# Two gated layers in one matmul stream: the second layer's tiles taken in turns with the first layer's later products

## The chip, the cores and the metric

The kernel runs on one NeuronCore of a Trainium2 chip. The metric is device time in microseconds (us) of one execution; lower is better. Engines are called as in the profile: PE (TensorE, the matrix engine), PEld (its weight loads), DVE (VectorE), ACT (ScalarE), POOL (GpSimd), SP (SyncE, which issues the DMAs here).

## The reference

Eight batches of 512 tokens with 512 features pass a gated feed-forward net twice: with weights of an expert that the batch's label picks, and with shared weights. The two results are mixed with two weights per batch and added to the input.

```python
def ffn(x, wi0, wi1, wo):                     # 512 -> 2048 -> 512
    return gelu(x @ wi0) * (x @ wi1) @ wo
share_out  = ffn(x, sWi0, sWi1, sWo)
expert_out = ffn(x, Wi0[label], Wi1[label], Wo[label])     # per batch
gate_in = concatenate([expert_out[:, 0], share_out[:, 0]])
w = softmax(relu(gate_in @ g0) @ g1)
return x + expert_out * w[:, 0] + share_out * w[:, 1]
```

All of it is float32.

## The kernel before

**Split operands.** A float32 operand is kept as a high part (a rounding to fp32r, made by ACT) and a low part (the rest, made by DVE as a difference). A product takes three passes: low by high, high by low, high by high (PASSES).

**Seven products.** The first layer (x by wi0, called GATE, and x by wi1, called LIN) is computed as a two-by-two block product with seven block products instead of eight (P1 to P7, in the order P5, P1, P6, P2, P7, P3, P4 of their storage). The sums of weight blocks that it needs are made by DVE (weight_sums, L948 to L956). The results are put together in PSUM and on DVE: c11 is P1 + P2; c22 and c12 are ps_v and ps_p5 with a saved P5 added (L1044, L1048); c21 is P4 on top of a copy of ps_v (copy_u, L821).

**Steps and passes.** The hidden width of 2048 is walked in 8 steps of 256. Batches go in pairs, and a pair is 24 steps: 8 expert steps of the first batch, 8 shared steps for both batches at once, 8 expert steps of the second batch. There are 4 pairs. An expert step is one turn, with matmuls 256 columns wide. A shared step has two turns, a GATE turn and then a LIN turn, with matmuls 512 columns wide (wide_product, L427): 6 of them in each product.

**Second layer.** What a step produced, the hidden block, is multiplied by wo one step later. Its four row tiles (down, L436) are 6 matmuls of 512 columns each, into the four banks of ps_outs. In the shared steps the GATE turn takes the tiles of one batch and the LIN turn those of the other (shared_tile); DVE adds each tile to s_out (add_tile, L1063). The first shared step of a pass still owes the last expert step's tiles; they go in its LIN turn (expert_tile), and ACT copies them out (L738).

**Before the hidden block can be used** in step n it must be split: DVE multiplies the last quarter that needs P4 of the LIN turn (c21_product, L1020), ACT makes the high part (hid_hi, L703), DVE the low part (hid_lo, L931, hidl), and that raises hid_ready. PE waits for hid_ready(n) in front of the first tile of the step.

**Order.** Each engine runs its own list, written out by hand, in order, with semaphores between the lists. For a LIN turn DVE's list is (shared_lin): c11 product, c22, c12, the product of act and lin (L1218), the low part of the next step's weights, group 0 (a_lo(n+1, 0), 128x2048), four adds, the low part of group 1 (a_lo(n+1, 1), 128x1024). For a GATE turn (shared_gate): c21_product of the turn before, weight_sums 0 and 1, hid_lo, weight_sums 2, a_lo of group 2, c22, c12, four adds, the low part of wo. P1 of a step waits for a_ready of group 0 of its weights. P7 waits for v_copied, a copy that ACT makes after P6, and P4 for u_copied, one that ACT makes after P7.

**On SP** the loads of weights (next_a, next_wo) wait for a_ready and wo_ready of the step, and load for the step two or one later.

Of the kernel before, what the change touches and what calls it, by code (L numbers as in the profile page):

```python
# [19 lines left out]
GATE, LIN = 0, 1  # L20
# [29 lines left out]
def first_turn(n):  # L50
    pair, q = divmod(n, PAIR_STEPS)
    return pair * PAIR_TURNS + (q if q < STEPS else 2 * q - STEPS if q < 2 * STEPS else q + STEPS)
# [25 lines left out]
def downs(t):  # L78


    return 4 * t - (4 if WIDE0 <= t % PAIR_TURNS < EXPERT1 else 0)
# [16 lines left out]
def a_splits(m, g):  # L98


    return 5 if m == 0 else m * 3 + (g + (5 if m == 1 else 6))
# [7 lines left out]
def x_splits(b, g):  # L109

    return 8 if b == 0 else b * 3 + (g + 6)


def build(nc, x_cols, x_rows, labels, experts, shared, g0_rows, g1_rows, out):
# [3 lines left out]
    MC = TOK // P  # L118
# [9 lines left out]
    with ExitStack() as ctx:  # L128
# [3 lines left out]
        def sem(name):  # L132
            return ctx.enter_context(nc.semaphore(name))
# [58 lines left out]
        def halves(ps):  # L192
            return ps.rearrange("p (a t) -> p a t", a=2)
# [23 lines left out]
        wo_ready = sem("wo_ready")  # L217
# [15 lines left out]
        hid_ready = sem("hid_ready")  # L233
# [177 lines left out]
        def _(pe):  # L411
# [11 lines left out]
            def wide_product(i, a, ps, start):  # L423

                for k in range(2):
                    for q, (ap, xp) in enumerate(PASSES):
                        mm = nc.tensor.matmul(ps, a_op[ap][:, i, a, k, :],  # L427
                                              x_op[xp][:, i, k, :, :].rearrange("p h t -> p (h t)"),
                                              start=(start and k == 0 and q == 0), stop=(k == 1 and q == 2),
                                              skip_group_check=True)  # L430
                return mm

            def down(m, s, start, stop, hidden):
                for f in range(2):
                    for q, (hp, wp) in enumerate(PASSES):
                        mm = nc.tensor.matmul(ps_out[m], hidden[hp][:, f, m * P:(m + 1) * P], wo[s][wp][:, f, :],  # L436
                                              start=(start and f == 0 and q == 0), stop=(stop and f == 1 and q == 2),
                                              skip_group_check=True)
                return mm
# [40 lines left out]
            def c11_taken(t):  # L480
                if is_gate(t):
                    pe.wait_ge(gelu_done, gelus(t) + 1)
                else:
                    pe.wait_ge(product_done, products(t) + 1)

            def expert_tile(m, b, n):

                c = n % STEPS
                start = c == 0
                if c == 0 and b == BATCH - 1:  # L490

                    pe.wait_ge(negative_copied, m + 1)
                    start = False
                elif c == 0 and b % 2 == 1:

                    pe.wait_ge(added, (b // 2 + 1) * PAIR_ADDS - MC + (m + 1))
                elif c == 0 and b > 0:

                    pe.wait_ge(out_copied, (b - 1) * MC + (m + 1))
                down(m, n % 2, start, c == STEPS - 1, hidden_of[0]).then_inc(down_done, 1)  # L500

            def shared_tile(m, h, b, n):

                row = n % STEPS * 2 + h
                if row == 0:

                    pe.wait_ge(out_copied, b * MC + (m + 1))
                else:

                    pe.wait_ge(added, b // 2 * PAIR_ADDS + row * MC - MC + (m + 1))  # L510
                down(m, n % 2, True, True, hidden_of[h]).then_inc(down_done, 1)
# [54 lines left out]
            def shared_turn(n, c, b, a):  # L566

                t = first_turn(n) + a
                if a == GATE:
                    pe.wait_ge(a_ready, a_splits(n, 0))  # L570
                    if c == 0:
                        pe.wait_ge(x_ready, x_splits(b + 1, 2))
                c11_taken(t - 1)
                wide_product(P1, a, ps_c11[:, :], True).then_inc(p_done[P1], 1)
                pe.wait_ge(c12_done, t - 1)
                wide_product(P5, a, ps_p5, True).then_inc(p_done[P5], 1)
                pe.wait_ge(p1_copied, t)
                wide_product(P6, a, ps_v, False).then_inc(p_done[P6], 1)
                wide_product(P2, a, ps_c11[:, :], False).then_inc(p_done[P2], 1)
                if a == GATE:  # L580
                    pe.wait_ge(a_ready, a_splits(n, 1))
                pe.wait_ge(v_copied, t)
                wide_product(P7, a, ps_v, False).then_inc(p_done[P7], 1)
                wide_product(P3, a, ps_p5, False).then_inc(p_done[P3], 1)

                if a == (GATE if c > 0 else LIN):
                    pe.wait_ge(hid_ready, n)
                    pe.wait_ge(wo_ready, n)
                for m in range(MC):
                    if c > 0:  # L590
                        shared_tile(m, a, b, n - 1)
                    elif a == LIN:
                        expert_tile(m, b, n - 1)
                if a == GATE:
                    pe.wait_ge(a_ready, a_splits(n, 2))
                pe.wait_ge(u_copied, t)
                wide_product(P4, a, ps_c21[:, :], False).then_inc(p_done[P4], 1)
# [19 lines left out]
            n, t, b = N_STEPS - 1, N_TURNS - 1, BATCH - 1  # L617
# [311 lines left out]
        def _(dve):  # L929
# [60 lines left out]
            def hid_lo(n):  # L990
                dve.wait_ge(hid_hi_done, n + 1)
                if is_wide(n):
                    lo(hs[LO][:, :, :, :], act[:, :, :, :], hs[HI][:, :, :, :], hid_ready)
                else:
                    lo(hs[LO][:, 0, :, :], act[:, LIN, :, :], hs[HI][:, 0, :, :], hid_ready)
# [17 lines left out]
            def c21_product(t):  # L1013

                if is_gate(t):
                    return
                if is_lin(t):
                    dve.wait_ge(gelu_done, gelus(t))
                    dve.wait_ge(p_done[P4], t)
                    nc.vector.tensor_tensor(act[:, :, 1, 0:HALF], act[:, :, 1, 0:HALF], halves(ps_c21[:, :]), ALU.mult  # L1020
                                            ).then_inc(product_done, 1)
                else:
                    dve.wait_ge(gelu_done, gelus(t) + 3)
                    nc.vector.tensor_tensor(act[:, LIN, 1, 0:HALF], act[:, GATE, 1, 0:HALF], ps_c21[:, HALF:2 * HALF],
                                            ALU.mult).then_inc(product_done, 1)
# [15 lines left out]
            def c22(t, to):  # L1041
                dve.wait_ge(u_copied, t)
                dve.wait_ge(p5_saved, t)
                nc.vector.tensor_tensor(to, halves(ps_v), p5[:, :, :], ALU.add).then_inc(c22_done, 1)  # L1044

            def c12(t, to):
                dve.wait_ge(p_done[P3], t)
                nc.vector.tensor_tensor(to, halves(ps_p5), p5[:, :, :], ALU.add).then_inc(c12_done, 1)  # L1048

            def add_tile(m, h, b, n, t, skip):  # L1050


                dve.wait_ge(down_done, downs(t) - skip - MC + (m + 1))
                to = s_out[:, h, m, :]
                if n % STEPS == 0:
                    if b > 0:

                        dve.wait_ge(out_stored, (b - 2 + h) * 16 + 16)
                    nc.vector.tensor_copy(to, ps_out[m]).then_inc(added, 1)
                else:  # L1060

                    dve.wait_ge(added, b // 2 * PAIR_ADDS + (n % STEPS * 2 + h - 2) * MC + (m + 1))
                    nc.vector.tensor_tensor(to, to, ps_out[m], ALU.add).then_inc(added, 1)  # L1063
# [128 lines left out]
            def shared_gate(n, c, b):  # L1192
                t = first_turn(n)
                c21_product(t - 1)
                weight_sums(n + 1, 0)
                weight_sums(n + 1, 1)
                hid_lo(n - 1)
                weight_sums(n + 1, 2)
                a_lo(n, 2)
                dve.wait_ge(hid_ready, n)  # L1200
                c22(t, act[:, :, 1, HALF:TOK])
                c12(t, act[:, :, 0, HALF:TOK])
                if c > 0:
                    for m in range(MC):
                        add_tile(m, 0, b, n - 1, t, 0)
                wo_lo(n)

# [188 lines left out]
```

## Time and profile before

| | |
|---|---|
| median of 3 runs | 1965.66 us (1965.66 to 1966.04) |
| span of the profiled execution, first to last instruction | 1964.4 us |
| PE busy | 1959.5 us, 11159 matmuls |
| DVE busy | 1525.0 us |
| ACT busy | 1038.3 us |
| POOL busy | 81.8 us |
| DMA, mean | 99 GB/s |

The profiled execution is known by its span; the 1.26 us between it and the median of the runs lie around the first and last instruction. Times in the trace are counted from the span's start. A matmul's duration in the trace has its pipeline's tail in it, so neighbours overlap: what a matmul costs is the distance from its start to the next one's. The same holds for other engines' instructions, which start up to 0.1 us before the one ahead ends.

### The profile page before, as it was taken

What the parts mean: (1) busy time and instruction counts of PE and PEld (TensorE: products, weight loads), DVE (VectorE), ACT (ScalarE), POOL (GpSimd) and SP (SyncE); (2) the same over time, 40 slices, a digit from 0 to 9 for tenths busy, and PEclk for the clock granted to TensorE, in tenths of its full rate; (3) what the DMA queues carried; (4) which work ended last, traced back from release to release, by engine and by line L of the source; (5) the groups of instructions that cost most, each with busy time, mean ns of one, the idle gap of its engine ahead of it and who ended that gap; (6) DMA issues with size and microseconds to landing.
All of it is one profiled execution on the core that took longest, in us unless ns stands there. A gap on an engine that the chain in (4) does not pass through costs nothing.

```text
span 1964.4 us, 29030 instructions
## 1 busy us (share of the span) xinstructions
PE 1959.5 (100%) x11159; PEld 1728.9 (88%) x11159; DVE 1525.0 (78%) x1814; ACT 1038.3 (53%) x1379; POOL 81.8 (4%) x56
## 2 busy tenths in 40 slices
PE   9999999999999999999999999999999999999999
PEld 8988888899998888889999888889999988888998
DVE  8776667789887676778988767668898876766888
ACT  6564444466666444446666644344666664434564
POOL 0000000001010000000201000000010100000000
PEclk9999999999999999999999999999999999999999
DMA  5431111244452111124445311112444421111243
GB/s 161 144 103 54 59 49 54 68 158 140 144 181 84 61 52 49 55 86 140 155 146 167 97 49 54 47 62 76 155 152 145 162 92 49 54 54 54 79 163 113
DMA packets 152428, 194.83 MB, mean 99 GB/s; under 512 B 10466, under 2 KB 116962, under 8 KB 150498
## 3 DMA queue, kind: packets, MB, share of 16 engines
q1 hardware_dynamic: 151746, 192.46, 30.2%
q8 instruction: 88, 1.44, 0.3%
q10 hardware_dynamic: 544, 0.52, 0.1%
q14 instruction: 50, 0.41, 0.1%
HBM read 184.55 MB, written 8.39 MB: 98 GB/s over the span
## 4 chain that ended last, share of the span: by engine, by line
PE 99%; DVE 1%; issue 0%; ACT 0%; DVEq 0%; ACTq 0%
PE ps_outs L436 35%; PE ps_pv L417 18%; PE ps_pv L427 18%; PE ps_c L417 13%; PE ps_c L427 13%; PE ps_c L458 0%; PE ps_pv L611 0%; DVE al L931 0%; PE ps_outs L417 0%; PE ps_outs L458 0%; PE ps_outs L445 0%; DVE a_src L952 0%; DVE xl L931 0%; DVE hidl L931 0%; DVE a_src L948 0%
## 5 line engine op out<-in xcount | busy, mean ns | idle before, releaser
L931 DVE TENSOR_TENSOR al<-a_src,ah 128x1024 fp32r<-128x1024 f32 (+3 forms) x293 | 402.0, 1374 | 34.3 <-ACT ah L659 33.7
L659 ACT CAST ah<-a_src 128x1024 fp32r<-128x1024 f32 (+2 forms) x285 | 334.9, 1187 | 0.5 <-DVE a_src L952 0.5
L417 PE MATMUL ps_pv<-xh,al 128*128 128x256 f32 x1008 | 285.4, 283 | 0.2 <-ACT ps_pv L815 0.2
L417 PE MATMUL ps_pv<-xl,ah 128*128 128x256 f32 x1008 | 285.3, 283 | 0.0
L417 PE MATMUL ps_pv<-xh,ah 128*128 128x256 f32 x1008 | 285.3, 283 | 0.0
L716 ACT ACTIVATE act<-ps_c 128x256 f32<-128x256 f32 (+1 forms) x191 | 87.1, 456 | 308.3 <-PE ps_c L417 170.6
L806 ACT COPY ps_pv<-ps_c 128x512 f32<-128x512 f32 x127 | 72.5, 571 | 268.0 <-PE ps_c L427 182.1
L417 PE MATMUL ps_c<-xh,ah 128*128 128x256 f32 x756 | 213.9, 283 | 0.0
L417 PE MATMUL ps_c<-xl,ah 128*128 128x256 f32 x756 | 213.9, 283 | 0.0
L417 PE MATMUL ps_c<-xh,al 128*128 128x256 f32 x756 | 213.6, 283 | 0.0
L436 PE MATMUL ps_outs<-wo0h,hidl 128*128 128x512 f32 x512 | 199.6, 390 | 0.0
L436 PE MATMUL ps_outs<-wo0l,hidh 128*128 128x512 f32 x512 | 199.6, 390 | 0.0
L427 PE MATMUL ps_pv<-xh,al 128*128 128x512 f32 x512 | 199.4, 389 | 0.0
L427 PE MATMUL ps_pv<-xl,ah 128*128 128x512 f32 x512 | 199.2, 389 | 0.0
L427 PE MATMUL ps_pv<-xh,ah 128*128 128x512 f32 x512 | 199.2, 389 | 0.0
L436 PE MATMUL ps_outs<-wo0h,hidh 128*128 128x512 f32 x512 | 199.2, 389 | 0.0
L1063 DVE TENSOR_TENSOR s_out<-s_out,ps_outs 128x512 f32<-128x512 f32 x224 | 146.1, 683 | 67.6 <-PE ps_outs L436 67.3
L436 PE MATMUL ps_outs<-wo1h,hidl 128*128 128x512 f32 x504 | 196.5, 390 | 0.0
L436 PE MATMUL ps_outs<-wo1l,hidh 128*128 128x512 f32 x504 | 196.4, 390 | 0.0
L436 PE MATMUL ps_outs<-wo1h,hidh 128*128 128x512 f32 x504 | 196.1, 389 | 0.0
L417 PEld LDWEIGHTS ps_pv<-xh,al 128*128 128x128 f32 x1008 | 193.5, 192 | 0.6 <-issue 0.5
L417 PEld LDWEIGHTS ps_pv<-xl,ah 128*128 128x128 f32 x1008 | 193.5, 192 | 0.1
(131 smaller groups left out, 3943.2 us busy)
## 6 DMA issues: line engine op xcount, KB each, us to landing
a_src<-experts SPq DMA_DIRECT2D x255, 256.0 KB, 3.7
raw_wo<-experts SPq DMA_DIRECT2D x128, 256.0 KB, 2.8
a_src<-shared SPq DMA_DIRECT2D x128, 256.0 KB, 3.0
g_sb<-g_rows SPq DMA_DIRECT2D x16, 1024.0 KB, 5.4
raw_wo<-shared SPq DMA_DIRECT2D x64, 256.0 KB, 2.8
x_src<-x_cols SPq DMA_DIRECT2D x30, 256.0 KB, 3.9
g_sb<-x_rows SPq DMA_DIRECT2D x7, 1024.0 KB, 4.8
out<-s_out SPq DMA_DIRECT2D x7, 1024.0 KB, 7.2
```

Of the source, the lines that this page charges most:

```text
L417: mm = nc.tensor.matmul(ps[:, a * HALF:(a + 1) * HALF], a_op[ap][:, i, a, k, :], x_op[xp][:, j, k, h, :], start=(start and a == 0 and k == ...
L427: mm = nc.tensor.matmul(ps, a_op[ap][:, i, a, k, :], x_op[xp][:, i, k, :, :].rearrange("p h t -> p (h t)"), start=(start and k == 0 and q ...
L436: mm = nc.tensor.matmul(ps_out[m], hidden[hp][:, f, m * P:(m + 1) * P], wo[s][wp][:, f, :], start=(start and f == 0 and q == 0), stop=(sto ...
L659: nc.scalar.copy(a_op[HI][:, i:j, :, :, :], a_src[m % 2][:, i:j, :, :, :]).then_inc(a_hi_done, 1)
L716: nc.scalar.activation(to, of, ACT.Gelu_apprx_tanh).then_inc(gelu_done, 1)
L806: nc.scalar.copy(ps_v, ps_c11[:, :]).then_inc(p1_copied, 1)
L931: nc.vector.tensor_tensor(to, of, hi.bitcast(F32), ALU.subtract).then_inc(done, 1)
L1063: nc.vector.tensor_tensor(to, to, ps_out[m], ALU.add).then_inc(added, 1)
```

## The change

In shared steps PE's order changes from P1 P5 P6 P2 P7 P3 T0 T1 T2 T3 P4 to P1 P5 P6 P2 **T0** P7 **T1** P3 **T2 T3** P4 (T0 to T3 are the tiles of the second layer; in the GATE turn of the first shared step of a pass there are none). The waits for hid_ready and wo_ready move with T0. DVE's list of a GATE turn takes the add of tile 0 between c22 and c12; its list of a LIN turn stays as it is.

```diff
+                def tile(m):
+
+                    if a == (GATE if c > 0 else LIN) and m == 0:
+                        pe.wait_ge(hid_ready, n)
+                        pe.wait_ge(wo_ready, n)
+                    if c > 0:
+                        shared_tile(m, a, b, n - 1)
+                    elif a == LIN:
+                        expert_tile(m, b, n - 1)
+
                 wide_product(P2, a, ps_c11[:, :], False).then_inc(p_done[P2], 1)
+                tile(0)
                 if a == GATE:
                     pe.wait_ge(a_ready, a_splits(n, 1))
                 pe.wait_ge(v_copied, t)
                 wide_product(P7, a, ps_v, False).then_inc(p_done[P7], 1)
+                tile(1)
                 wide_product(P3, a, ps_p5, False).then_inc(p_done[P3], 1)
-
-                if a == (GATE if c > 0 else LIN):
-                    pe.wait_ge(hid_ready, n)
-                    pe.wait_ge(wo_ready, n)
-                for m in range(MC):
-                    if c > 0:
-                        shared_tile(m, a, b, n - 1)
-                    elif a == LIN:
-                        expert_tile(m, b, n - 1)
+                tile(2)
+                tile(3)
                 if a == GATE:
                     pe.wait_ge(a_ready, a_splits(n, 2))
                 pe.wait_ge(u_copied, t)
@@ shared_gate, on DVE
                 c22(t, act[:, :, 1, HALF:TOK])
+                if c > 0:
+                    add_tile(0, 0, b, n - 1, t, 0)
                 c12(t, act[:, :, 0, HALF:TOK])
                 if c > 0:
-                    for m in range(MC):
+                    for m in range(1, MC):
                         add_tile(m, 0, b, n - 1, t, 0)
                 wo_lo(n)
```

## Rows read from the trace of the kernel before

**Rows 1.** The page: PE's busy time, and its granted clock in 40 slices.

```profile
PE 1959.5 (100%) x11159; PEld 1728.9 (88%) x11159; DVE 1525.0 (78%) x1814; ACT 1038.3 (53%) x1379; POOL 81.8 (4%) x56
...
PEclk9999999999999999999999999999999999999999
```

**Rows 2.** Waits of PE: waiting line, releaser, us in total, times, longest.

```profile
PE ps_pv L611 <- DVE idle L1280: 1.2, 1, 1.2
PE ps_pv L417 <- ACT ps_pv L815: 0.2, 1, 0.2
```

**Rows 3.** Timeline of PE, a LIN turn and the next GATE turn: start, duration.

```profile
226.00 0.39 PE L427 MATMUL ps_c<-xh,al 128*128 128x512 f32 x1
...
233.94 0.39 PE L427 MATMUL ps_pv<-xh,ah 128*128 128x512 f32 x1
234.16 0.39 PE L436 MATMUL ps_outs<-wo0h,hidl 128*128 128x512 f32 x1
...
240.96 0.39 PE L427 MATMUL ps_c<-xh,al 128*128 128x512 f32 x1
...
246.40 0.39 PE L427 MATMUL ps_pv<-xh,al 128*128 128x512 f32 x1
...
249.12 0.39 PE L436 MATMUL ps_outs<-wo1h,hidl 128*128 128x512 f32 x1
```

**Rows 4.** Timeline of DVE in the same stretch.

```profile
234.36 0.69 DVE L1048 TENSOR_TENSOR lin<-ps_pv,p 128x512 f32<-128x512 f32 x1
235.14 1.23 DVE L1218 TENSOR_TENSOR act<-act,lin 128x1024 f32<-128x1024 f32 x1
236.29 2.28 DVE L931 TENSOR_TENSOR al<-a_src,ah 128x2048 fp32r<-128x2048 f32 x1
238.49 2.47 DVE L1063 TENSOR_TENSOR s_out<-s_out,ps_outs 128x512 f32<-128x512 f32 x4
240.88 1.22 DVE L931 TENSOR_TENSOR al<-a_src,ah 128x1024 fp32r<-128x1024 f32 x1
242.01 0.68 DVE L1020 TENSOR_TENSOR act<-act,ps_c 128x512 f32<-128x512 f32 x1
...
243.33 1.22 DVE L952 TENSOR_TENSOR a_src<-a_src 128x1024 f32<-128x1024 f32 x1
244.95 2.29 DVE L931 TENSOR_TENSOR hidl<-act,hidh 128x2048 fp32r<-128x2048 f32 x1 [0.40 <-ACT hidh L703]
```

**Rows 5.** Timeline of ACT in the same stretch.

```profile
243.00 1.91 ACT L703 CAST hidh<-act 128x2048 fp32r<-128x2048 f32 x1
...
247.34 0.60 ACT L716 ACTIVATE act<-ps_c 128x512 f32<-128x512 f32 x1 [0.74 <-DVE hidl L931]
```

**Rows 6.** Timeline of all engines where PE's weight load waits for ACT.

```profile
138.20 0.59 ACT L806 COPY ps_pv<-ps_c 128x512 f32<-128x512 f32 x1
...
138.84 0.19 PEld L427 LDWEIGHTS ps_pv<-xh,al 128*128 128x128 f32 x1 [0.20 <-ACT ps_pv L806]
138.90 0.44 PE L427 MATMUL ps_pv<-xh,al 128*128 128x512 f32 x1
```

**Rows 7.** Timelines of ACT and DVE, second shared step of a pass, GATE turn.

```profile
152.76 0.57 ACT L806 COPY ps_pv<-ps_c 128x512 f32<-128x512 f32 x1 [2.13 <-PE ps_c L427]
153.24 1.91 ACT L703 CAST hidh<-act 128x2048 fp32r<-128x2048 f32 x1
```

```profile
155.19 2.29 DVE L931 TENSOR_TENSOR hidl<-act,hidh 128x2048 fp32r<-128x2048 f32 x1 [1.17 <-ACT hidh L703]
```

**Rows 8.** Timelines of PE and DVE in the first expert step after a shared pass.

```profile
360.64 0.28 PE L417 MATMUL ps_c<-xh,al 128*128 128x256 f32 x1
...
369.27 0.40 PE L436 MATMUL ps_outs<-wo1h,hidl 128*128 128x512 f32 x1
```

```profile
364.70 2.29 DVE L931 TENSOR_TENSOR hidl<-act,hidh 128x2048 fp32r<-128x2048 f32 x1 [0.47 <-ACT hidh L703]
```

**Rows 9.** Timeline of PE at the start of the kernel.

```profile
1.18 4.88 PE L611 MATMUL ps_pv<-idle 128*128 128x512 bf16 x11 [1.18 <-DVE idle L1280]
```

## The prediction

> **What bounds the kernel now.** I read four views. The page says that PE is busy for all but 5 us of the span, at full granted clock in every slice [rows 1]. Busy time alone proves little, since a matmul's record overlaps the next, so I took the list of PE's waits: 1.4 us in all, 1.2 of it before the first matmul [rows 2]. Then the timeline of PE in a shared step: P1 of the LIN turn starts at 226.00, P1 of the next GATE turn at 240.96 [rows 3]. A turn has 7 products and 4 tiles, 11 blocks of 6 matmuls, so 66 matmuls take 14.96 us, 0.2267 us each and 1.36 us a block, and every start that I read is on that grid. There is no idle time in these turns to win. The total of late starts over the whole kernel is under 5 us, most of it in the first step; in the shared passes it is four times about 0.05 us, once a pass [one of them in rows 6]. The question is therefore only which of the waits that now pass unnoticed becomes late. The timelines of DVE and ACT answer it [rows 4, 5].
>
> **What the change moves on PE.** No matmul is added or removed, and no DMA. P7 goes one block later, P3 two blocks later (2.72 us), T0 two blocks earlier, T1 one block earlier; T2, T3 and P4 keep their places. T0 carries the wait for hid_ready with it.
>
> **Slack of the two waits that matter, before.** (1) P1 of the GATE turn needs a_lo of group 0. It ends at 236.29 + 2.28 = 238.57 [rows 4], P1 starts at 240.96 [rows 3]: 2.39 us of slack. (2) T0 of the GATE turn needs hid_lo, which ends at 244.95 + 2.29 = 247.24 [rows 4]; T0 starts at 249.12 [rows 3]: 1.88 us of slack.
>
> **What P3 two blocks later does to DVE.** c12 reads P3's result. It starts at 234.36, 0.42 us after P3's last matmul at 233.94 [rows 3, 4]. (The instruction before it ends at about the same time, so the true delay could be a little less; I take 0.42 and so move c12 by the full 2.72 us.) Nothing in DVE's list after c12 has any idle time ahead of it down to c21_product: the product of act and lin starts 0.78 us after c12, a_lo of group 0 1.15 us after that, the four adds 2.20 us later, a_lo of group 1 2.39 us later, c21_product 1.13 us later [rows 4]. DVE takes a list in order, so all of them move by 2.72 us:
>
> a_lo of group 0 ends at 238.57 + 2.72 = 241.29. P1 can follow 0.11 us later: that is the distance from the end of ACT's copy (138.20 + 0.59 = 138.79) to the matmul that waited for it (138.90), with the weight load between at 138.84 [rows 6]. So P1 starts at 241.40 in place of 240.96, **0.44 us late**.
>
> The tiles that the adds read are there in time: T3 still ends its block at 239.60 (one block before 240.96), and the adds now start at 241.21. a_lo of group 1 then starts at 243.60, c21_product at 244.73, ending 245.41. ACT's high part can start 0.10 us after that (the hop of DVE's end at 247.24 to ACT's start at 247.34 [rows 4, 5]): 245.51. Before, it started at 243.00, when ACT had copied P1; that copy now starts at P1 + 1.56, 242.96, and is no obstacle. The high part takes 1.91 us [rows 5], to 247.42, hid_lo follows 0.04 us later, at 247.46 (weight_sums 1, which is ahead of it in DVE's list, ends at 243.33 + 1.22 + 2.72 = 247.27 [rows 4], in time), and ends at 249.75. T0 can start at **249.86**.
>
> **What T0 two blocks earlier asks for.** On the old grid T0's new place is 246.40, where P7 was [rows 3]. So from a grid without stalls PE is 249.86 - 246.40 = **3.46 us** behind when T0 starts, the 0.44 us of P1 in it; the stall in front of T0 itself is 3.02 us. Both moves eat the same slack: 2.72 us for the tile, 2.51 us for the chain (2.72 less 0.21 that ACT's copy had cost it), 0.11 us of hop, against 1.88 us.
>
> **Does it repeat?** Each step makes its own delay: the chain hangs on P3 of its own LIN turn, so a lost stretch is not made good, nor does a delay excuse the next. From T0 of the GATE turn, T0 P7 T1 P3 T2 T3 P4 and then P1 P5 P6 P2 T0 P7 T1 P3 of the LIN turn are 15 blocks, 20.40 us; the rest of the loop is the chain, from P3's last start 13.20 us to T0, less the 0.23 us of that matmul's own pitch. Together 33.37 us a step, where 22 blocks are 29.92.
>
> **Other waits of the longer step.** Everything else is behind T0 with room. v_copied: ACT's list has the P5 copy and the P6 copy behind the high part, so P6's copy ends near 248.6; P7 is at 251.2. u_copied for P4: P7 ends near 252.6 and its copy 0.8 us later; P4 is at 258.0. c12 of the GATE turn ends near 256.2 and is needed by P5 at 260.7. The add of tile 0 between c22 and c12 costs 0.6 us of DVE in a place where DVE waits for P3 anyway, and the other three wait for T2 and T3 as before; I cost this edit at nothing. If c12 had no cover it would cost 0.6 us at most, with 4 us of room until P5. SP's loads run one to two steps ahead and wait for the same semaphores, 3.5 us later in a step that is 3.5 us longer. The wait in front of T0 holds back P7 and P3 of the same turn, and through them ACT's copy and DVE's c22 and c12; they return to PE only at P4 and at the next turn's P5, whose room is given above.
>
> **The ends of a pass.** In the first shared step of a pass the LIN turn has tiles but DVE adds none, so the chain is 2.39 us shorter. There hid_lo waits for ACT, and ACT for P1's copy: copy at 152.76, high part at 153.24, hid_lo 155.19 to 157.48 [rows 7]. P1 of that GATE turn was at 152.76 - 1.56 = 151.20. It goes 0.44 us later by the same a_lo, copy and split move along, hid_lo ends at 157.92, T0 starts at 158.03 and its place was 151.20 + 4 blocks = 156.64: **1.39 us**. After the last shared step the first expert step has its old order. Its P1 is late by 0.44 us. Its tiles come 8.63 us behind P1 (360.64 to 369.27), so at 369.71; hid_lo ends at 364.70 + 2.51 + 2.29 = 369.50, plus 0.11 [rows 8]. It just fits: **0.44 us**.
>
> **The sum.** A pass has 8 shared steps: 1.39 once, 3.46 six times (GATE turns of the third to the eighth step), 0.44 once: 22.59 us. Four passes: 90.4 us. On the span: 1964.4 + 90.4 = 2054.8; with the 1.26 us around it, and so against the median, **2056 us**. Unknown sizes: the start of c12 after P3 (0.42 us, or as little as 0.3 if DVE itself was the last to come free), the hop to PE (0.11, between 0.05 at the load and 0.2), and hops inside the chain, about 0.1 us each way. Together some 0.3 us a step over 28 steps, 8 us: 2048 to 2064 for this case.
>
> **Rivals.** *The clock falls.* PE now stands 3.02 us in front of 24 tiles, which no place of the old trace shows in midstream. Against it: the granted clock is full in all slices [rows 1]. For it: at the start 11 matmuls of 512 columns take 4.88 us, that is (4.88 - 0.63)/10 = 0.425 us each, the pitch of the 1.2 GHz level, nearly twice the 0.2267 of the turns [rows 9]; so the lower level exists right after idleness, and 11 matmuls at it cost about 2.2 us over. If each of the 24 stalls brought that back, 24 x 2.2 = 52 us come on top, since the stalled stretch lies in the loop: 2109 us. It decides whether 3 us of standing is enough. The Trainium skill, TensorE: Matmul & The Clock Gate, "HAM oscillation — how this bites in real kernels", warns that gaps between bursts of matmuls make the clock fall back to half rate, again in every turn of a loop; by that rule this rival would be the outcome, while no gap in this trace tests it. PE would still work through 30 of each 33.4 us and has shown the full clock throughout, so I give this rival 8 in 100.
>
> *Only the tile's own move counts.* Were the later c12 absorbed by idle time in DVE's list (there is some ahead of each LIN turn), hid_lo would stay at 247.24 and T0 wait 0.95 us for 246.40, in 28 GATE turns: 27 us, 1992 us. For it speaks that DVE is busy only 78% of the time [rows 1]; against it that the idle time lies before c12 and not behind it [rows 4]. 4 in 100; values between this one and the forecast, by some overlap that I don't see, 4 more.
>
> *Not slower.* The one thing that the new order loosens is P7's wait for v_copied, by a block. It would decide if the split of the hidden block kept clear of T0, which needs 3.46 us less of chain, more than all four adds take (2.39 us). Then PE stays on its grid, and at most the four late starts of rows 6 go with it: 1965.5 us. The rows leave no place for such a saving: 3 in 100.
>
> *A longer step than thought*, some wait of the chain that I cost at nothing (ACT's list behind the late high part is the candidate), 1 us a step more: 2084 us, 5 in 100.
>
> **Numbers.** Forecast 76 in 100. The range takes in its own, and widens on both sides to 2040 and 2076 for half of the near cases; what is left out is the clock, the two low rivals and half of the longer step. Under 0.2% (3.9 us) is what this kernel's measurement can hardly tell from no change. Slower by more: 96; within: 3; faster: 1, since only 0.2 us of waits are there to be removed.
>
> **What the profile after should show.** PE waiting in front of T0 of 24 GATE turns, about 3.0 us each, with DVE's hid_lo as releaser; about 1 us in 4 more; and 0.44 us in front of P1 in 32 places. Steps of 33.4 us. PE's busy time as before, DVE's and ACT's too. In DVE's timeline, c12 of the LIN turn 2.7 us later against P1 of its turn, with nothing idle behind it until c21_product. The prediction is wrong if hid_lo's chain starts before P3's end, if the stall is at P7 or P4, or if matmuls after a stall go at 0.43 us.

## The result, and the profile after

The changed kernel takes 2076.87 us (median of 4 runs, 2075.08 to 2086.61); the kernel before took 1965.85 us beside it. The ratio is 1.0575, with a 95% interval of 1.056 to 1.0589. The forecast was slower, 2056 us with a range of 2040 to 2076: the direction and most of the size came, but the time lies 0.9 us above the range. Three of the four runs lie between 2075 and 2079 us at a mean granted clock of 0.992 or 0.993, the fourth at 2086.61 us and 0.988. The profiled execution of the changed kernel has a span of 2073.5 us, 109.1 us more than before.

The page of the changed kernel: PE's busy time against [rows 1], the slices, and the chain that ended last, by engine.

```profile
span 2073.5 us, 29030 instructions
PE 1990.3 (96%) x11159; PEld 1732.8 (84%) x11159; DVE 1518.8 (73%) x1814; ACT 1043.1 (50%) x1379; POOL 79.6 (4%) x56
PEclk9999999999999999999999999999999999999999
PE 81%; DVE 14%; ACT 3%; issue 2%; DVEq 0%; ACTq 0%
```

The instructions are the same in number, and DVE and ACT are as busy as before. But the chain now runs through DVE and ACT for 17% of the span, and PE's busy time *rose* by 31 us though it does the same 11159 matmuls. Part of it is slow matmuls (below, 11 us); the rest are the modelled tails in front of each stall and the longer records behind it. The clock digits don't show the slow ones: each is an average over 52 us, and 9 means 90% or more. The mean granted clock over the whole execution is 0.993; it was 1.000.

PE's waits in the changed kernel, against [rows 2] (waiting line, releaser, us in total, times, longest):

```profile
PEld ps_outs L436 <- DVE hidl L936: 78.1, 28, 3.1
PE ps_outs L436 <- DVE hidl L936: 66.3, 28, 2.7
...
PEld ps_c L427 <- DVE al L936: 18.1, 28, 0.6
...
PE ps_c L427 <- DVE al L936: 6.2, 28, 0.2
...
PE ps_pv L417 <- ACT ps_pv L820: 5.1, 4, 1.3
...
PEld ps_c L417 <- DVE al L936: 2.6, 4, 0.6
```

A weight load (PEld) waits from the end of the load before it, a matmul from the modelled end of its neighbour, so one stall stands in both rows with two lengths and is not to be added. The first pair is the forecast stall in front of T0, 28 times, released by hid_lo. The second pair, with the last row, is the forecast stall in front of P1, 28 + 4 times. The PE row released by ACT's L820, four times 1.3 us, was not forecast.

The same loop as in [rows 4], one step of the changed kernel on DVE:

```profile
245.92 0.69 DVE L1053 TENSOR_TENSOR lin<-ps_pv,p 128x512 f32<-128x512 f32 x1 [1.37 <-PE ps_pv L427]
246.70 1.23 DVE L1225 TENSOR_TENSOR act<-act,lin 128x1024 f32<-128x1024 f32 x1
247.84 2.28 DVE L936 TENSOR_TENSOR al<-a_src,ah 128x2048 fp32r<-128x2048 f32 x1
250.04 2.47 DVE L1068 TENSOR_TENSOR s_out<-s_out,ps_outs 128x512 f32<-128x512 f32 x4
252.44 1.22 DVE L936 TENSOR_TENSOR al<-a_src,ah 128x1024 fp32r<-128x1024 f32 x1
253.57 0.68 DVE L1025 TENSOR_TENSOR act<-act,ps_c 128x512 f32<-128x512 f32 x1
...
256.23 2.29 DVE L936 TENSOR_TENSOR hidl<-act,hidh 128x2048 fp32r<-128x2048 f32 x1
```

and on PE, the timeline of the same step (the matmul ahead of the stall, T0, and P7):

```profile
250.18 0.50 PE L427 MATMUL ps_c<-xh,al 128*128 128x512 f32 x1 [0.22 <-DVE al L936]
...
255.54 0.39 PE L427 MATMUL ps_c<-xh,ah 128*128 128x512 f32 x1
258.57 0.80 PE L436 MATMUL ps_outs<-wo1h,hidl 128*128 128x512 f32 x1 [2.65 <-DVE hidl L936]
259.17 0.63 PE L436 MATMUL ps_outs<-wo1l,hidh 128*128 128x512 f32 x1
259.59 0.63 PE L436 MATMUL ps_outs<-wo1h,hidh 128*128 128x512 f32 x1
...
261.30 0.52 PE L427 MATMUL ps_pv<-xh,al 128*128 128x512 f32 x1
261.66 0.39 PE L427 MATMUL ps_pv<-xl,ah 128*128 128x512 f32 x1
```

c12 (245.92) now shows PE as its releaser, 0.43 us behind P3's last matmul at 245.49; from there to c21_product nothing on DVE has any idle time. T0 starts 12.65 us after c12, where the forecast had 12.78 (249.86 less 237.08), and P1 to P1 of two GATE turns takes 33.43 us (216.75 to 250.18), where it had 33.37. That is the loop as forecast. But behind this T0 the matmuls come 0.42 us apart, 259.17 to 259.59: that is the 1.2 GHz level. The windows view of 2.5 us behind two stalls of the same length, one step apart, shows it in the granted clock (the column behind POOL):

```profile
225.00:227.50 2.50, 2.36 (x10) 1.95 (x11) 1.29 (x3) 0.60 (x1) 0.00 (x0) 1.00 0.03 9
258.50:261.00 2.50, 2.42 (x6) 1.96 (x7) 1.22 (x3) 0.60 (x1) 0.00 (x0) 0.50 0.04 12
```

Ten matmuls at 1.00 in the first, six at 0.50 in the second. In this execution 8 of the 24 long stalls have such a stretch behind them, and they are not scattered: of the six long stalls of a pass it is the third and the fifth in each of the four passes (258.57 and 326.8 in the first, 774.0 and 842.2 in the second). The next P1 is then 34.80 us behind instead of 33.43 (250.18 to 284.98): 1.37 us each.

**Where the 109 us are.** From the start times of all matmuls against their pitch: P1 32 x 0.38 = 12.3; T0 in all 70.8 (24 x 2.80 and 4 x 0.88); P7 of the first expert step 5.8; slow stretches 8 x 1.4 = 11; and some 9 us of restarts, since the second matmul after a stall is also late, by 0.11 us, and the next few by 0.01. Sum 109.

### The profile page after: what moved, and what is told of

Same layout as the page of the kernel before. It is cut to its first block, busy times and chain, and to the rows that moved or that the text cites. A ratio compares the mean times of both kernels' runs of the same rounds, so it can differ in the third digit from the quotient of the medians.

```text
span 2073.5 us, 29030 instructions
## 1 busy us (share of the span) xinstructions
PE 1990.3 (96%) x11159; PEld 1732.8 (84%) x11159; DVE 1518.8 (73%) x1814; ACT 1043.1 (50%) x1379; POOL 79.6 (4%) x56
## 4 chain that ended last, share of the span: by engine, by line
PE 81%; DVE 14%; ACT 3%; issue 2%; DVEq 0%; ACTq 0%
PE ps_outs L436 30%; PE ps_pv L417 17%; PE ps_pv L427 13%; PE ps_c L417 13%; PE ps_c L427 7%; DVE al L936 5%; DVE hidl L936 3%; ACT hidh L708 3%; DVE s_out L1068 3%; DVE lin L1053 1%; DVE act L1025 1%; DVE s_out L1064 0%; DVE act L1225 0%; PE ps_c L458 0%; PE ps_pv L616 0%
## 5 line engine op out<-in xcount | busy, mean ns | idle before, releaser
L664 ACT CAST ah<-a_src 128x1024 fp32r<-128x1024 f32 (+2 forms) x285 | 338.3, 1188 | 10.8 <-PE ps_pv L427 10.3
L436 PE MATMUL ps_outs<-wo1h,hidl 128*128 128x512 f32 x504 | 202.2, 401 | 31.7 <-DVE hidl L936 31.7
L826 ACT COPY ps_c<-ps_pv 128x512 f32<-128x512 f32 x126 | 71.9, 571 | 247.3 <-PE ps_pv L427 194.7
L417 PEld LDWEIGHTS ps_pv<-xh,ah 128*128 128x128 f32 x1008 | 193.5, 192 | 0.0
```

Of the source, the lines that this page charges most:

```text
L417: mm = nc.tensor.matmul(ps[:, a * HALF:(a + 1) * HALF], a_op[ap][:, i, a, k, :], x_op[xp][:, j, k, h, :], start=(start and a == 0 and k == ...
L664: nc.scalar.copy(a_op[HI][:, i:j, :, :, :], a_src[m % 2][:, i:j, :, :, :]).then_inc(a_hi_done, 1)
L826: nc.scalar.copy(ps_c21[:, :], ps_v).then_inc(u_copied, 1)
```

## The experiments

All times are medians of 4 runs; in each set before ran beside them (1965.76 to 1966.03 us). "Slow stretches" counts, in the profiled execution, the long stalls with matmuls at the 0.43 us pitch behind them.

| kernel | us | ratio (95%) | mean clock | slow stretches |
|---|---|---|---|---|
| changed, again | 2088.10 | 1.0622 (1.0604 to 1.064) | 0.988 | 15 of 24 |
| lin_plain | 1994.83 | 1.0148 (1.0131 to 1.0165) | 1.000 | no long stall |
| gate_plain | 2032.50 | 1.034 (1.0323 to 1.0358) | 1.000 | no long stall |
| adds_behind | 2020.68 | 1.0279 (1.0262 to 1.0296) | 1.000 | no long stall |
| filler | 2064.16 | 1.05 (1.0482 to 1.0517) | 1.000 | none |
| longer_stall | 2156.83 | 1.0972 (1.0953 to 1.099) | 0.965 | 24 of 24 |
| last_lin_plain | 2078.19 | 1.0572 (1.0555 to 1.059) | 0.987 | 14 of 24 |
| dve_list_old | 2089.25 | 1.0613 (1.0576 to 1.065) | 0.987 | 15 of 24 |
| filler_last_lin | 2055.85 | 1.0458 (1.044 to 1.0475) | 1.000 | none |
| filler_dve_list | 2063.98 | 1.0499 (1.0481 to 1.0516) | 1.000 | none |

**1. Each half of the move alone.** In lin_plain the LIN turns have PE's old order, in gate_plain the GATE turns have it (and DVE's list of the GATE turn its old order):

```diff
+                plain = a == LIN          # gate_plain: a == GATE
                 wide_product(P2, a, ps_c11[:, :], False).then_inc(p_done[P2], 1)
-                tile(0)
+                if not plain:
+                    tile(0)
...
-                tile(1)
+                if not plain:
+                    tile(1)
                 wide_product(P3, a, ps_p5, False).then_inc(p_done[P3], 1)
+                if plain:
+                    tile(0)
+                    tile(1)
```

> LIN turns in the old order, GATE turns in the new one. Two-term theory: hid_lo ends as before the change, T0 asks for it 2.72 us earlier with 1.88 us of slack, so PE waits about 1 us in 28 GATE turns and nowhere else; 28 us over before, 1994 us, no wait at P7 of the expert step. Together with the run with plain GATE turns this is far less than the 111 us of the whole change, because the slack is then there twice. Rival (the loss is that of the earlier T0 alone, whatever P3 does): above 2050 us.

Measured 1994.83 us, 1 us from the expectation. The waits of lin_plain (28 at T0, none of P1 or P7):

```profile
PEld ps_outs L436 <- DVE hidl L942: 32.4, 28, 1.2
...
PE ps_outs L436 <- DVE hidl L942: 20.6, 28, 0.7
```

So the earlier T0 by itself costs 29 us; this is 1.0 us for each of 28 stalls, the 2.72 us of the move less the 1.88 us of slack, plus the restart.

> GATE turns in the old order on PE and DVE, LIN turns in the new one. Two-term theory (the later c12 of the LIN turn and the earlier T0 of the GATE turn eat the same slack of hid_lo): the chain still runs about 2.5 us late, T0 stands at its old place with 1.9 us of slack, so PE waits 0.5 us in front of each P1 after a LIN turn (32 times), some 0.25 us in front of T0 (24 times), and 1.5 us at P7 of the first expert step (4 times): about 28 us over before, 1993 us. No stall is long, so no slow matmuls. Rival (only the tile's own move counts): within 3 us of before, 1966 us.

Measured 2032.50 us, 39.5 us more than expected. The stalls at P1 are there as expected. In front of T0 there is none, because PE already stood at P7 (waits of gate_plain):

```profile
PE ps_pv L427 <- ACT ps_pv L826: 37.1, 24, 1.6
...
PE ps_c L427 <- DVE al L942: 6.2, 28, 0.2
...
PE ps_pv L417 <- ACT ps_pv L826: 5.2, 4, 1.3
```

The timeline of all engines around one of the 24 shows what releases it:

```profile
185.17 0.68 DVE L1031 TENSOR_TENSOR act<-act,ps_c 128x512 f32<-128x512 f32 x1
...
185.89 1.92 ACT L714 CAST hidh<-act 128x2048 fp32r<-128x2048 f32 x1 [1.84 <-DVE act L1031]
...
187.13 0.39 PE L427 MATMUL ps_c<-xh,ah 128*128 128x512 f32 x1
...
187.70 0.58 ACT L821 COPY p<-ps_pv 128x512 f32<-128x512 f32 x1
...
188.37 0.57 ACT L826 COPY ps_pv<-ps_pv 128x512 f32<-128x512 f32 x1
...
189.08 0.47 PE L427 MATMUL ps_pv<-xh,al 128*128 128x512 f32 x1 [1.57 <-ACT ps_pv L826]
```

ACT takes its list in order. It waits 1.84 us for c21_product, makes the high part, then the P5 copy, then the P6 copy, and that last one is v_copied, which P7 needs. In the changed kernel's shared steps T0 stands between P2 and P7 and waits longer still, so this wait does not show; take T0 away and it costs 1.7 us. I had checked v_copied only with T0 in front of P7. The late chain has three consumers, not two.

This spoils one test that the expectation of lin_plain had set. The halves cost 29 and 67 us; together that is not far less than the whole change but near the 98 us that it costs with the clock held up (experiment 4), because the unforeseen wait at P7 fills the difference. And gate_plain can't say whether the late chain alone makes T0 wait, since PE comes to T0 late already. That the two moves eat one slack is read from the length of the stall at T0: from the starts of the matmuls it is 0.90 us with the chain on time (lin_plain) and 2.80 us with the chain late.

**2. The wait at P7 of the first expert step.** That step has no tile ahead of P7 either. last_lin_plain is the change with `plain = a == LIN and c == STEPS - 1`: the last LIN turn of each pass in the old order, so that the chain into the expert step is on time.

> The whole change, but the last LIN turn of each pass in the old order. If the 1.4 us wait at P7 of the first expert step comes from ACT, which makes the late high part of the hidden block ahead of the copy that P7 waits for, it goes, and so does the 0.5 us wait of P1: 4 x 2 = 8 us less than the changed kernel, 2068 us. Rival (the wait at P7 is the first expert step's own, by its narrower products): only the 0.5 us goes, 2075 us.

The time, 2078.19 us, says nothing here: this kernel had 14 slow stretches, 6 more than the changed kernel's first profile. In its trace the waits at P7 are gone, and 28 of the 32 at P1 are left (10.8 us for 12.3). With the clock held up by the filler of experiment 4 the same edit can be read from the time:

> The kernel with filler matmuls and, beside them, the last LIN turn of each pass in the old order; the filler keeps the clock up, so that the small difference can be read from the time. If P7 of the first expert step waits for a copy that ACT makes behind the late high part, the four waits of 1.45 us and the four of 0.5 us at P1 go: 8 us less than the filler kernel's 2064.2, 2056 us. Rival (that wait belongs to the expert step itself): 2062 us.

2055.85 us against 2064.16 for the filler kernel, 8.3 us less; 8 were expected. The wait belongs to the late chain and not to the expert step. Its rows in the changed kernel, all engines, first expert step:

```profile
390.70 1.91 ACT L708 CAST hidh<-act 128x2048 fp32r<-128x2048 f32 x1 [1.79 <-DVE act L1025]
...
392.34 0.28 PE L417 MATMUL ps_c<-xh,ah 128*128 128x256 f32 x1
392.52 0.57 ACT L815 COPY p<-ps_pv 128x512 f32<-128x512 f32 x1
...
393.18 0.57 ACT L820 COPY ps_pv<-ps_pv 128x512 f32<-128x512 f32 x1
393.66 0.62 ACT L664 CAST ah<-a_src 128x512 fp32r<-128x512 f32 x1
393.89 0.36 PE L417 MATMUL ps_pv<-xh,al 128*128 128x256 f32 x1 [1.27 <-ACT ps_pv L820]
```

**3. The chain shortened.** adds_behind moves three of the four adds of a LIN turn behind the next hid_lo; the results are the same.

```diff
 # shared_lin
-                    for m in range(MC):
+                    for m in range(MC if c == STEPS - 1 else 1):
                         add_tile(m, 1, b, n - 1, t, 0)
 # shared_gate
                 hid_lo(n - 1)
+                if c > 1:
+                    for m in range(1, MC):
+                        add_tile(m, 1, b, n - 2, t - 1, 0)
```

> The changed kernel with three of the four adds of a LIN turn moved behind the next hid_lo in VectorE's list (all steps but the last of a pass): the chain to hid_lo is 3 x 0.6 = 1.8 us shorter. Chain theory: the stall in front of T0 falls from 3.0 to 1.2 us in 24 GATE turns, and at that length no clock falls: 24 x 1.8 = 43 us plus some 11 us of clock less than the changed kernel, 2021 us. Rival (the stall is set by something other than VectorE's list, as ACT's high part or PE's own order): little change, above 2060 us.

Measured 2020.68 us, on the expectation. DVE's timeline has one add left between the two low parts, and T0's stall is 1.0 us:

```profile
212.20 2.28 DVE L936 TENSOR_TENSOR al<-a_src,ah 128x2048 fp32r<-128x2048 f32 x1
214.40 0.68 DVE L1068 TENSOR_TENSOR s_out<-s_out,ps_outs 128x512 f32<-128x512 f32 x1
215.00 1.22 DVE L936 TENSOR_TENSOR al<-a_src,ah 128x1024 fp32r<-128x1024 f32 x1
```

**4. The clock.** filler puts 12 matmuls of the idle tile, whose result T0 overwrites, into the place of the long stall; longer_stall puts two more DVE operations into the chain, on a scratch tile.

```diff
 # filler
+FILL = 12
 # in tile(m)
+                    if a == GATE and c > 1 and m == 0:
+                        pe.wait_ge(added, b // 2 * PAIR_ADDS + (n - 1) % STEPS * 2 * MC - MC + 1)
+                        for i in range(FILL):
+                            nc.tensor.matmul(ps_out[0], idle[:, 0:P], idle[:, :], start=True, stop=True)
 # longer_stall, in shared_gate, ahead of hid_lo
+                if c > 1:
+                    dve.wait_ge(hid_hi_done, n)
+                    for i in range(2):
...
+                        nc.vector.tensor_tensor(extra[:, :], act[:, 0, 0, :], act[:, 1, 0, :], ALU.subtract
+                                                ).then_inc(extra_done, 1)
```

> The changed kernel with 12 matmuls of the idle tile (bf16, 512 columns, zeros) into the bank of tile 0 ahead of the wait for hid_ready, in the 24 GATE turns with the long stall; they add nothing to the result. They take 12 x 0.21 = 2.6 us of a stall of 3 us, so they cost no time of their own. If the slow matmuls behind 8 of 24 stalls come from PE's standing, all go: about 8 x 1.4 = 11 us less than the changed kernel, 2065 us, granted clock 1.00. Rival (they come from something else at that place, as the load of the weights or the tile's operands): as the changed kernel, 2076 us, clock 0.99.

Measured 2064.16 us, and the four runs lie within 0.5 us where the changed kernel's spread over 11. T0 is released when it was before (225.20 in this trace, 225.14 in the changed kernel's); only the slow matmuls behind it are gone. The timeline of PE and the windows view over all passes:

```profile
222.38 2.76 PE L585 MATMUL ps_outs<-idle 128*128 128x512 bf16 x12
225.20 0.50 PE L437 MATMUL ps_outs<-wo0h,hidl 128*128 128x512 f32 x1
```

```profile
126.00:2040.00 1914.00, 1897.82 (x10481) 1619.54 (x10481) 1395.65 (x1656) 957.29 (x1254) 71.66 (x46) 1.00 0.29 92
```

> The changed kernel with two more VectorE differences of 128x512 into a scratch tile ahead of hid_lo in the 24 GATE turns: the chain is 1.5 us longer, the stall 4.5 us in place of 3.0. If standing makes the clock fall, more of the 24 stalls have slow matmuls behind them, perhaps all: 24 x 1.5 = 36 us for the chain and up to 16 x 1.4 = 22 us for the clock, up to 2134 us, clock near 0.98. Rival (slow stretches have nothing to do with the length of the stall): 8 of 24 as before, 2112 us.

All 24 stalls, now 4.4 us between the matmuls' starts, have a slow stretch, and the clock was 0.965. The time is 2156.83 us, 23 more than the upper expectation: in 20 of the 24, all but the first of each pass, the slow stretch is also longer, 11 to 13 matmuls and about 2.7 us over instead of 6 or 7 and 1.4. The chain itself costs 32 us more (4.13 us of gap for 2.80), and 20 x 2.7 + 4 x 1.4 = 60 us of clock on the filler kernel's 2064 make 2156. PE's timeline behind one of these stalls:

```profile
229.99 0.79 PE L438 MATMUL ps_outs<-wo0h,hidl 128*128 128x512 f32 x1 [3.99 <-DVE hidl L938]
...
232.28 0.63 PE L438 MATMUL ps_outs<-wo0h,hidh 128*128 128x512 f32 x1
232.71 0.63 PE L429 MATMUL ps_pv<-xh,al 128*128 128x512 f32 x1
...
234.42 0.63 PE L429 MATMUL ps_pv<-xl,ah 128*128 128x512 f32 x1
```

> The changed kernel, nothing altered, for a second profile. If the slow stretches depend on where a stall falls in time and not on the program, their number differs from the first profile's 8 of 24, and the time with it by 1.4 us each, between 2064 us (none) and 2098 us (all); the stalls themselves are as in the first profile. Rival (they belong to certain steps of the program): the same 8, in the same steps, 2075 us.

Measured 2088.10 us with 15 slow stretches, in other steps than the first time: behind the T0 at 225.45 there was one now, where the first profile had none at 225.14. Again they keep to places: the second, fourth and sixth long stall of each pass, and in three passes the first too. The stalls are the same (12.3 us at P1, 70.9 at T0, 5.8 at P7). So the number of slow stretches is a matter of the execution, and the changed kernel's median moves with it: 2076.87 us in one set of runs, 2088.10 in another. Executions of one set differ too: the four of dve_list_old below had a mean clock of 0.993 once (2076.91 us) and of 0.985 to 0.987 three times (2087.86 to 2091.25 us). What makes an execution take one pattern or the other no run here shows.

**5. DVE's edit.** dve_list_old has PE's new order and DVE's old list.

> The whole change on PE, VectorE's list as before it (add of tile 0 behind c12). My theory: that edit lies where VectorE waits for P3 and is worth nothing: the changed kernel's time within 5 us (the number of slow stretches differs between executions). Rival: the add delays c12 by 0.6 us and gives some of it back, several us lower.

2089.25 us with 15 slow stretches: no verdict, the clock's scatter covers it. Again the filler settles it:

> The kernel with filler matmuls and, beside them, VectorE's list as before the change; again the filler takes the clock's scatter out. My theory: the place of the add of tile 0 is worth nothing, 2064.2 us, within 1 us. Rival: it is worth several us, one way or the other.

2063.98 us against 2064.16, no difference. The edit is worth nothing either way.

## Why the prediction was wrong, step by step

**Right: the bound, and no gain.** PE had nothing to win. No kernel of the set came below 1994 us.

**Right: the two terms and the loop.** Forecast for them: 90.4 us. The kernel with filler, in which nothing else is left but the waits at P7 (6 us), is 98.4 us over before; with the last LIN turn plain too, 89.8 us, where the same sum without its four P1 stalls gives 88.6. The size per step was 33.37 us forecast and 33.43 measured. That the two moves eat one slack is shown by the stall at T0: 0.90 us where only T0 moved (lin_plain), 2.80 us where the chain is late as well, and 1.0 us again when three adds are taken out of the late chain (adds_behind). gate_plain adds nothing to this, since its wait at P7 comes first.

**Wrong: "The clock falls" as a rival of 8 in 100, all or nothing.** This is the step that failed, and most of the miss. The text priced it at all 24 stalls or none (2109 or 2056 us). It came in 8 of 24 in the profiled execution and in 15 of 24 in another, at 1.4 to 1.6 us each and not 2.2: 11 us in the first, some 22 in the other. The forecast had this term at nothing. That standing causes it is shown from both sides: with matmuls in the stall's place none of 24 is left (filler), with a longer stall all 24 come (longer_stall). The Trainium skill, TensorE: Matmul & The Clock Gate, "HAM oscillation — how this bites in real kernels", speaks of gaps between bursts that throttle the clock again in every turn of the loop; the loop of its example stands longer than it works. Of the loops here, which work far longer than they stand, the trace agrees for longer_stall (24 of 24), and for the changed kernel it shows a mixture (granted clock 0.50 behind one stall, 1.00 behind the next). My ground for 8 in 100, that PE works through 30 of each 33.4 us, was no evidence: what went before the stall did not help in longer_stall either.

**Wrong: "Everything else is behind T0 with room", for the first expert step.** In "The ends of a pass" I followed hid_lo to the tiles and found it just in time, which it was (no stall there). I did not follow ACT's list, where the copy for P7 stands behind the late high part. Four waits of 1.45 us, 6 us, shown by filler_last_lin. The rival "A longer step than thought" named ACT's list as candidate, but priced it as 1 us in every step; it was 1.5 us in four places.

**Sum.** 2056 + 6 + 11 = 2073 us, and some 2 us of restarts (a stall at P1 costs 0.5 us with its late second matmul, where I had 0.44) bring it to the 2075 us of the profiled execution. A range moved up by either term would have held the time; that it was missed by 0.9 us and not by ten is luck, since the second set of the same kernel came at 2088.10 us.

**Right: the added costs at nothing.** DVE's edit, SP's loads, u_copied and c12 of the GATE turn have no wait of PE in the trace.

## What to carry to other kernels

When PE is full, an interleaving can only use up slack, so list the slack of each wait before the change: an operation that moves later and a consumer that moves earlier are charged to the same account if a chain joins them. Follow a late instruction through every engine's ordered list, past the consumer you care about, and do it again for each step with another order (here the first step of the next pass). Where a forecast puts a stall of about 3 us into every turn of a matmul loop, as here, price a clock that falls in a part of them, and look at single windows, since slices and a mean clock of 0.99 hide it.

## What the hardware showed that I had not expected

Two executions of one program gave 8 and 15 slow stretches out of 24 equal stalls, which spreads the time over 14 us where a kernel without them repeats within 0.5 us. Within an execution they come nearly at the same places of each pass: the third and fifth of six stalls in one, the second, fourth and sixth, and mostly the first, in the other. The lower level behind a stall of 3 us lasted 6 to 8 matmuls of 512 columns, but 13 behind one such stall in last_lin_plain and one in dve_list_old; behind one of 4.4 us it lasted 8 in the first stall of each pass and 11 to 13 in the others. And 12 matmuls on a tile of zeros, 2.76 us in all, in the stall's place kept the granted clock at 1.00 in all 24: the kernel is 12.7 to 24 us shorter with them than with PE standing. Shortening the stall is worth far more (adds_behind: 56 us under the changed kernel's first median, by three adds moved in a list).
